# Softmax denominators of the upper 256 query columns: added up on POOL, then one product on PE

## What is computed

```python
scores = jnp.einsum('bhir,bhjr->bhij', q_lr, k_lr) * scale
causal_mask = jnp.triu(jnp.ones((Tq, Tq), dtype=bool), k=1)
scores = jnp.where(causal_mask, jnp.float32(-jnp.inf), scores)
attn = jax.nn.softmax(scores, axis=-1)
y = jnp.einsum('bhij,bhjd->bhid', attn, v)
...
x = _layernorm(x + _L0_attn_ref(...), axis=-1)
```

## Time and profile before

| | |
|---|---|
| runs (us) | 4101.57, 4103.56, 4105.52; median 4103.56 |
| profiled execution | 4101.11, of which the span is 4099.4 |
| attention | about 125 to 2330 us of the span |
| PE busy, whole span | 3733.7 us (91%) |
| DVE busy | 2260.1 us (55%) |
| ACT busy | 1477.0 us (36%) |
| POOL busy | 659.9 us (16%) |
| mean granted clock of PE | 0.949 of full speed |
| `y_bank` products (L686) | 332.5 us busy |
| `den_bank` products (L686) | 320.2 us busy |

### The profile page before, as it was taken

How to read it: one execution, slowest core, us unless ns; L and a number is a source line. 1 busy time by engine, 2 the same in 40 slices (tenths; PEclk the granted TensorE clock), 3 DMA queues, 4 the chain that set the end, 5 groups by cost and what they waited for, 6 DMA issues and landing times. The chain is left out here.

```text
span 4099.4 us, 57478 instructions
## 1 busy us (share of the span) xinstructions
PE 3733.7 (91%) x21481; PEld 2562.6 (63%) x21481; DVE 2260.1 (55%) x3998; ACT 1477.0 (36%) x2756; POOL 659.9 (16%) x853
## 2 busy tenths in 40 slices
PE   5899999999999999999999814799999999999994
PEld 3555555555555555555555314688888888888883
DVE  2565565664665655656646457444454444445455
ACT  1343443443443434434434301233333333333334
POOL 2021121121121211211211200011111111111112
PEclk8999999999999999999999955799999999999997
DMA  5234233143322342341433100334344443434457
GB/s 161 49 97 130 58 91 117 43 109 99 96 71 84 104 117 71 81 127 43 109 99 73 53 21 6 121 115 126 105 132 126 123 126 105 126 117 124 139 168 273
DMA packets 189688, 423.61 MB, mean 103 GB/s; under 512 B 39841, under 2 KB 42913, under 8 KB 181537
## 3 DMA queue, kind: packets, MB, share of 16 engines
q1 hardware_dynamic: 162800, 367.97, 29.4%
q0 software_dynamic: 14400, 35.14, 4.4%
q10 hardware_dynamic: 12288, 17.83, 1.5%
HBM read 246.75 MB, written 72.38 MB: 78 GB/s over the span
## 5 line engine op out<-in xcount | busy, mean ns | idle before, releaser
L849 DVE TENSOR_REDUCE max_slots<-shared_banks 128x1 f32<-128x512 f32 (+3 forms) x1536 | 768.2, 549 | 404.1 <-PE shared_banks L625 328.5
L795 ACT ACTIVATE probs<-scores_t 128x512 f32<-128x512 f32 (+3 forms) x1536 | 662.8, 498 | 669.1 <-PE scores_t L667 615.7
L1684 PE MATMUL m_ps_y<-m_w_parts,m_hidden_parts 128*128 128x512 f32 x3072 | 739.5, 391 | 10.0 <-DVE m_hidden_parts L1595 9.5
L1684 PE MATMUL m_ps_h<-m_tokens_t,m_w_parts 128*128 128x512 f32 x3072 | 740.5, 391 | 1.6 <-DVE m_tokens_t L1566 1.6
L1684 PEld LDWEIGHTS m_ps_y<-m_w_parts,m_hidden_parts 128*128 128x128 f32 x3072 | 576.6, 188 | 136.5 <-issue 11.4
L1684 PEld LDWEIGHTS m_ps_h<-m_tokens_t,m_w_parts 128*128 128x128 f32 x3072 | 576.0, 188 | 120.0 <-issue 2.0
L667 PE MATMUL scores_t<-q_operands,k_operands 128*128 128x512 f32 (+3 forms) x1536 | 516.3, 393 | 39.0 <-ACT probs L795 30.7
L622 PE MATMUL shared_banks<-k_operands,q_operands 96*128 96x512 f32 (+3 forms) x1536 | 512.0, 387 | 32.9 <-DVE max_slots L849 13.8
L1503 ACT ACTIVATE m_hidden<-m_ps_h,m_b 128x512 f32<-128x512 f32 x256 | 176.4, 689 | 784.3 <-PE m_ps_h L1684 771.1
L527 POOL TENSOR_SCALAR_AFFINE_SELECT probs<-probs 128x256 f32<-128x256 f32 x512 | 219.0, 431 | 1424.2 <-ACT probs L795 1421.4
L622 PEld LDWEIGHTS shared_banks<-k_operands,q_operands 96*128 96x128 f32 x1536 | 296.0, 195 | 214.8 <-issue 138.0
(11 more groups left out here) (215 smaller groups left out, 3135.1 us busy)
## 6 DMA issues: line engine op xcount, KB each, us to landing
m_w_raw<-in_w1T SPq DMA_DIRECT2D x64, 1024.0 KB, 5.1
m_w_raw<-in_w2T SPq DMA_DIRECT2D x64, 1024.0 KB, 7.4
q_operands<-natural SPq DMA_DIRECT2D x384, 128.0 KB, 2.5
k_operands<-natural SPq DMA_DIRECT2D x384, 128.0 KB, 2.5
wqk_group<-scratch_wqk SPq DMA_DIRECT2D x32, 1024.0 KB, 5.2
natural<-in_xT SPq DMA_DIRECT2D x8, 2048.0 KB, 9.3
x_residual<-in_x ACTq DMA_DIRECT2D x64, 256.0 KB, 2.8
scratch_x<-probs SPq DMA_DIRECT2D x64, 256.0 KB, 2.1
```

What stands on the lines that cost most here:

```text
L795: act.activation(probs[:, slot_of(k, h // 2), h % 2, c0:HALF], st[:, (HG * k + h) % SCORE_BANKS, c0:HALF], ACT.Exp, scale=SCALE).then_inc( ...
L849: dve.tensor_reduce(mx[:, h, slot:slot + 1], src[:, 0:n], AX.X, ALU.max).then_inc(bank_free[bank], 1)
L1684: mm = pe.matmul(bank, a, b, start=(first and n == 0), stop=(final and n == len(pairs) - 1))
```

## The change

The 512 columns of a half are cut in two. For the lower 256 `sums` goes on as before, over those steps that reach them (`has_lower`: 8 of the 12), and ends at column 256. For the upper 256 POOL adds the exponentials of all steps of the half, element by element, in `acc`: one tile [128, 2, 256] for each pair of heads (a copy in the first step, an addition in the others). After the last step of a half PE multiplies each head's accumulator once with ones (`upper`), and the denominators' copy on DVE waits for that. `acc` of pair 0 lies in the second residual tile, so the load of that tile moves from step 8 to the start of the tail; space comes from a smaller `ln_stats` and a single `logits_half`. ACT's exponentials wait, in addition, until POOL has added the step that used the buffer before. The inversions of half 1 move from n = 0, 4, 4, 5 to n = 4, 5, 6, 7 of the group after; `upper` stands at n = 25 for half 0 and at n = 2 of the group after for half 1 (in the last group behind item ("out", 0)).

```diff
-INVERT_AFTER = ((30, 42, 45, 45), (0, 4, 4, 5))
+INVERT_AFTER = ((30, 42, 45, 45), (4, 5, 6, 7))
+UPPER = HALF // 2
+UPPER_AFTER = (25, 2)
...
+        acc = (xres[:, 1].rearrange("p (h n) -> p h n", h=2), sb("prob_sums", [P, 2, UPPER])[:])
-        stats = sb("ln_stats", [P, TT, 6])
+        stats = sb("ln_stats", [P, 2, 6])
-        logits = sb("logits_half", [P, 2, P])
+        logits = sb("logits_half", [P, P])
...
+            def add_probs(b, g, k, pair):
+                hh, j, c0 = steps[k]
+                s = (b * GROUPS + g) * NE + k
+                c = max(c0, UPPER)
+                src, total = probs[:, slot_of(k, pair), :, c:HALF], acc[pair][:, :, c - UPPER:UPPER]
+                if not diagonal[k]:
+                    plain(pool, exp_done, HG * s + 2 * pair + 2 + SCORE_BANKS, pool_passed)
+                if j == 0:
...
+                    if pair == 0 and s > 0:
+                        plain(pool, den_full, 2 * (b * GROUPS + g) + hh, pool_passed)
+                    pool.tensor_copy(total, src).then_inc(added, 1)
+                else:
+                    if diagonal[k]:
+                        plain(pool, masked, (b * GROUPS + g) * N_DIAG + masked_through(k) - 1 + pair, pool_passed)
+                    plain(pool, added, 2 * (s - 1) + pair + 1, pool_passed)
+                    pool.tensor_tensor(total, total, src, ALU.add).then_inc(added, 1)
...
                     if item[0] == "scores" and diagonal[item[2]] and item[3] % 2 == 1:
                         mask_probs(b, item[1], item[2], item[3] // 2)
+                    if item[0] == "scores" and item[3] % 2 == 1:
+                        add_probs(b, item[1], item[2], item[3] // 2)
...
-                        weigh(item[2], db, lambda h, j: ones[:]).then_inc(pv_done, 1)
+                        if has_lower(item[2]):
+                            weigh(item[2], db, lambda h, j: ones[:], UPPER, 1).then_inc(pv_done, 1)
...
+            def upper(b, g, hh):
+                n = 2 * (b * GROUPS + g) + hh
+                pe.wait_ge(added, 2 * ((b * GROUPS + g) * NE + last_step(hh) + 1))
+                pe.wait_ge(den_drained, n)
+                for h in range(HG):
+                    mm = pe.matmul(db[h * DH:(h + 1) * DH, UPPER:HALF], ones[:], acc[h // 2][:, h % 2, :],
+                                   start=True, stop=True, tile_position=(0, h * DH))
+                mm.then_inc(den_full, 1)
...
                     elif kind == "out":
                         r = item[1] % 2
+                        if item[1] == 0:
+                            load_residual(b, 1)
...
+                if h % 2 == 0 and s >= 2:
+                    act.wait_ge(added, 2 * (s - 2) + h // 2 + 1)
                 act.activation(probs[:, slot_of(k, h // 2), h % 2, c0:HALF], st[:, (HG * k + h) % SCORE_BANKS, c0:HALF],
...
-                    if ends_half(item):
-                        n = 2 * (b * GROUPS + item[1]) + steps[item[2]][0]
-                        dve.wait_ge(pv_done, (b * GROUPS + item[1]) * NE + item[2] + 2)
+                    if kind == "upper":
+                        n = 2 * (b * GROUPS + item[1]) + item[2]
+                        dve.wait_ge(den_full, n + 1)
                         dve.wait_ge(normed, n + 1)
                         dve.tensor_copy(den[:], db[:]).then_inc(den_drained, 1)
```

More of the change, by code:

```diff
@@ L243, in plan_tail @@
         if t == 0:
+            order.append(("upper", GROUPS - 1, 1))
             order += [("invert", GROUPS - 1, 1, i) for i in range(DEN_PIECES)]
@@ L325, in build_attention @@
         x_in, x_split, w_in = sem("x_in"), sem("x_split"), sem("w_in")
[L326 removed]
+        x_hi, added, den_full = sem("x_hi"), sem("added"), sem("den_full")
         hi_ready, first_hi = sem("hi_ready"), sem("first_hi")
@@ L345, in build_attention @@
         lead_in = plan_lead()
-        uses_bank = lambda item: item[0] not in ("scores", "values", "sums", "invert")
+        uses_bank = lambda item: item[0] not in ("scores", "values", "sums", "upper", "invert")
         diagonal = [j * P >= hh * HALF for hh, j, _ in steps]
```

45 lines of the change are left out of this document (32 added, 13 removed).

## The result

The changed kernel takes **4109.7 us** (median of 12 runs) against 4101.95 of the kernel before in the same session: a ratio of 1.0018, 95% interval 1.0009 to 1.0026. It is slower by a hair; forecast were 60 us less. The profiled execution has a span of 4111.6 us against 4099.4.

The account below looks back on a forecast made before the run. PE was taken to set the pace in the attention (busy 2117 of 2205 us). The terms -139 + 35 + 34 + 10 gave -60 us, so 4044 us, with a forecast of 4005 to 4075 and a range of 3965 to 4100.

Parts of the forecast that it names:

- Sums removed, products added: PE in attention: narrower `den_bank` sums less the added `upper` products save 4.47 or 3.98 us a group, 139 in all.
- POOL's new queue: Group starts: PE waits for POOL's second mask of step 2, behind copies and additions; together 35 us.
- the wait of 1.4 us at step 2: PE at the values of step 2, waiting for POOL's mask: 1.4 us, 24 times.
- DVE behind POOL: Before `maxT`: DVE's copy blocked by POOL's addition, PE waits 1.1 us (ends 0.65 and 2.5) in 31 places: 34 us.
- The split: Input split in 7 batches: DVE's additions take turns with POOL's, 1.5 us more each (ends 0 and 3): 10 us.
- the sign of the forecast: Whole kernel: 60 us less; chances faster 0.82, same 0.08, slower 0.10.
- The rivals: POOL keeps up (0.15), DVE loses the port each time (0.15), additions slower than their twin (0.10), change not as stated (nothing).
- the additions are slower than their twin: Rival: POOL's additions exceed `normalise`'s 1.28 us; gain gone from 1.75, 4135 us at 2.0; chance 0.10.
- ACT did wait for `added`: ACT's new wait for POOL's addition of the step two back: claimed met everywhere.
- `upper` never waited: The `upper` product on PE: the prediction would be wrong if it waits for POOL.
- the reductions kept their 0.59 us: DVE's reductions: the prediction would be wrong if they grow longer beside POOL.
- The ends of the unknown costs: Copies -10 and +8, own waits -12 and +8, port -14 and +43, split -10 and +10: 3998 to 4113 us.

Follow-up runs that it names:

- first: Changed kernel with POOL's additions cut to one column of each head, added sums left out, all waits and products kept: 4065.5 us, 0.9904.
- fifth run: Change in 55 of 64 halves, plus POOL masking both pairs before adding at diagonal steps and maxima joined without a copy: 4039.2 us, 0.9855.
- twelfth run: Kernel before, with DVE's two subtractions of the input done twice in the 7 batches with an input split: 4127.6 us, 1.0061.
- thirteenth run: Changed kernel with the next batch's input loaded early in four transfers and additions cut to one column: 4030.7 us, 0.9820.
- fourth run: Change in 55 of 64 halves; the 7 halves with an input split and the last batch's group 3 keep sums on PE: 4068.7 us, 0.9922.
- fourteenth run: Change in 55 halves with masks first, no copy, strips started by head, and early input in four transfers: 4025.9 us, 0.9809.
- seventh run: Changed kernel, all 64 halves, with the next batch's input loaded ahead of the next weights in four transfers: 4096.6 us, 0.9990.
- ninth: Change in 55 halves with masks first, no copy, and a head's strips started after that head's last score: 4042.8 us, 0.9854.
- eighteenth run: Kernel before, all sums on PE, with no copy, strips by head, early input, projections and join moved: 4087.3 us, 0.9957.

## Why the prediction was wrong

**Sums removed, products added** (-139): the sizes held. `den_bank` fell by 131 us. Where POOL costs nothing (first and fifth run) half 1 gains 2.43; the working gives 3.48 - 0.53 = 2.95. Of the other 0.5, 0.2 are in the last two sets: from the values of step 10 to the next score PE takes 1.44 us before (1048.33 to 1049.77) and 0.79 after (1043.02 to 1043.81), which is 0.65 less and not 0.85. The rest I can't place.

**POOL's new queue** (+35): the durations and the length of the chain held. From the start of the first mask (1045.69) to the end of the second mask of step 2 (1054.57 + 0.40) it is 9.28 us; forecast were 9.4. An own wait is 0.28 and not 0.1, a copy 0.04 shorter than taken. The own wait falls on the three additions of the chain, where I had counted five instructions. The rule of the Trainium skill, "GPSIMD Engine Reference", section "Performance versus the Vector engine", makes 0.44 us of the copy's 512 elements (an estimate from its 1.03 cycles each); it measured 0.61, and the measurement decides. The additions tell what is missing: 0.72 us for 256 elements and 1.27 for 512 leave 0.17 at none (an estimate, a straight line through the two), and 0.44 + 0.17 is the copy's 0.61. But the wait of 1.4 us at step 2 was mostly not met, since PE had already lost 1.27 to the strips 5 us earlier. That the size of the term came out nearly right is luck, since its cause was mostly another: taking POOL's part away (fifth run) brought 0.25 a group and not 1.4. The step that failed is that I followed only the engines that the change touches. SP's chain from DVE's part of the last projection to the first maxima, of which the last 5.6 us, from SP's first transfer on, are the same before and after, was full already (0.20 us of waiting in the row of before), and every sum removed between its two ends is worth nothing.

**DVE behind POOL** (+34): the mechanism held, the size was 0.6 to 0.7 and not 1.1. After an addition DVE's copy goes next:

```profile
356.90 1.27 POOL L562 TENSOR_TENSOR x_residual<-x_residual,probs 128x512 f32<-128x512 f32 x1 [0.28 <-ACT probs L857]
357.02 1.18 DVE L918 COPY row_max<-max_slots 128x16 f32<-128x16 f32 x1
...
358.12 0.16 DVE L919 TENSOR_TENSOR row_max<-max_slots 128x16 f32<-128x16 f32 x1
...
358.33 0.29 PE L668 MATMUL shared_banks<-ident_f,row_max 128*32 128x128 f32 x1 [0.59 <-DVE row_max L919]
```

The copy starts 0.12 us behind the addition and ends 0.03 behind it, and the mask of 358.12 comes after: that is the lower end of my range. The fifth run, with masks first and without the copy, gave 0.74 in each half 1.

**The split** (+10): **this term was mis-sized, 43 in place of 10** (+30.0 measured where the sums alone should have brought -13), and with it the sign of the forecast. I had counted one more of POOL's subtractions, 1.5 us. DVE's last subtraction ends 3.3 us later instead (11.70 us behind ACT's first part, not 8.37), and the twelfth run shows that 2.5 us of that alone cost 22 us in the 7 halves. Of the 3.3, 1.1 go with the additions' length (first and thirteenth run: 14 to 16 us of the 43); 2.3 stay with additions of 0.20 us and go only where the halves have no additions at all (fourth and fourteenth run). The failed reading is thus of POOL's order: I had its subtractions start a little later, and they came to stand behind additions that wait for exponentials. The rest is the input's transfer, which does not come earlier when PE does: in the 7 halves PE's wait for ACT grew from 10.1 to 18.4 us. The 21 us that the early input brings (seventh run) are no measure of it, since it brings 18 where the sums stay on PE (ninth against fourteenth run), and with it on both sides the 7 halves are 25 us longer with the change than without (+9.2 and -16.2, seventh and eighteenth run, the latter with further edits) instead of 30. Last, the clock: 22 us in slower products over the 7 halves, at 0.87 instead of 0.955, which overlaps with these and was nowhere in the working.

**The last batch** (nothing in the forecast): in its group 3 PE has no maxima and no projections between the scores, so nothing covers POOL:

```profile
2317.39 1.08 PE L738 MATMUL y_bank<-probs,v_rows 128*32 128x256 f32 x8 [0.64 <-POOL probs L541]
2320.66 0.66 PE L738 MATMUL y_bank<-probs,v_rows 128*32 128x128 f32 x8 [2.19 <-POOL probs L541]
```

A set of 256 columns takes 1.08 us in the first of these rows, not 0.64: in the 20 us up to the last drain the granted clock is 0.79 (1.00 in the kernel before). 12 us of miss; the fourth run, with the sums of this group on PE, took 5 of it, and with masks first (fifth) the two halves were down to +1.1. I had read one boundary and taken it for all.

**Behind the last drain**: 8 us of miss that no step spoke of. 3.9 are in the last batch's tail, why stays open; 4.6 are in the experts' stage, see below.

**The rivals.** None came as written. That the additions are slower than their twin was excluded (722 to 1293 ns). ACT did wait for `added`, against my count, 30 times and 47 us in all, but PE's wait for ACT stayed the same (30.8 and 30.7 us); `upper` never waited, and the reductions kept their 0.59 us; no gain at all, as in my slow-addition case, came about by another way, the split above all. The ends of the unknown costs, all taken together, had reached 4113; the range of 3965 to 4100 was narrower than my own working.

## What to carry to other kernels

When work leaves the bounding engine, list for each stretch which chains end at it with little or no slack, the DMA queues' too; what is removed between the ends of such a chain is worth nothing there. Look at the irregular places (input loads, last iterations) one by one, since the typical row does not speak for them. And where an engine takes on new work, put what others wait for ahead of it and leave out the places where it is already busy: here that turned +0.2% into -2.2%, of which 0.4% come from edits that help the kernel before as well. So try each remedy on the kernel before too: a gain that it brings there is no part of what the change had cost.

## What the runs showed of the hardware

**Code loading in a stage that was not changed.** The experts' stage, from its first to its last rows turned, took 1313.9 us before and 1318.5 after (from start to start). In all 20 profiles it is 1313.6 to 1314.4 in 13 and 1317.6 to 1318.5 in 7, and these 7 are those whose instruction queue shows 177 packets; the others show 123 to 127. The difference comes in six waits of up to 0.9 us, 179 us apart; the queue's row, and PE's wait in the changed kernel, 2560 to 4060 us:

```profile
q8 instruction: 177, 2.90, 0.3%
```

```profile
PE m_ps_h L1746 <- issue: 4.5, 6, 0.9
```

The kernel before has no such wait, and 126 packets. In its trace the queue moves nothing from 163 to 1264 us into this stage; in the changed kernel it moves some 9 packets in each 179 us of that time, and each of the six waits (the first at 191.8) ends 3 us behind one (188.7). The seven have the sums of 62 to 64 halves on POOL, so more of its instructions. That a loop then has to be loaded again in every round is what the packets suggest; which instructions bring it about was not tried. Between versions of one kernel, 4 us (0.1%) can be this.

**A wait for POOL's own instruction** costs 0.28 us: 362 waits of the additions for masks sum to 102.8 us, and both the shortest and the median one are 0.28.

**The port.** In the Trainium skill, "SBUF — State Buffer", section "Who interferes with whom", DVE and POOL share a pair of ports, which DVE's instructions of two SBUF inputs and copies in certain modes use, and which one engine then holds while the other blocks. The trace agrees and shows the turns: DVE's copy of 16 elements, which needs 0.17 us, takes 1.18 behind an addition of 1.27, and DVE's two subtractions of 1024 columns take 6.26 us beside POOL's two and a mask, where they took 3.32.
